# B and C rows of a selective scan: a BF16 scratch, two DMA queues, and an earlier dt

## What is computed

```python
xz = ln(x) @ in_proj_w.T
x_ssm, z = split(xz)                      # 2048 x 2048 each
xc = silu(causal_conv4(x_ssm) + conv_b)
xp = xc @ x_proj_w.T                      # one dt column, 16 of B, 16 of C
dt = softplus(xp[dt] * dt_proj_w + dt_proj_b)
dA = exp(dt * A)                          # 16 states per channel
h_t = dA_t * h_(t-1) + dt_t * B_t * xc_t  # along the 2048 time steps
y_t = sum over the 16 states of h_t * C_t
x = x + ln((y + xc * D) * silu(z) @ out_proj_w.T)
```

## Time and profile before

| | us |
|---|---|
| median of 3 runs | 8227.46 |
| lowest, highest | 8202.73, 8426.81 |
| the profiled execution | 8207.39 |
| its span on the slowest cores (2 and 4) | 8205.8 |
| its span on the fastest core (5) | 8162.0 |

### The profile page before, as it was taken

How to read it: one execution, slowest core, us unless ns; L and a number is a source line. 1 busy time by engine, 2 the same in 40 slices (tenths; PEclk the granted TensorE clock), 3 DMA queues, 4 the chain that set the end, 5 groups by cost and what they waited for, 6 DMA issues and landing times.

```text
span 8205.8 us, 45336 instructions; the slowest of 8 cores (8162.0 to 8205.8 us)
## 1 busy us (share of the span) xinstructions
PE 2813.7 (34%) x10928; PEld 1131.5 (14%) x11136; DVE 3911.4 (48%) x5726; ACT 1984.8 (24%) x2902; POOL 338.7 (4%) x639
## 2 busy tenths in 40 slices
PE   6200011001100020002605666666665645647272
PEld 3000000000000000001202222222221212223131
DVE  7199945996299917995212222122211343331414
ACT  4132212332133212332203333333331000011112
POOL 0100010001000010000000000000000000000000
PEclk9655556555655565555858777777776777768686
DMA  2600062001600070002691111111111111111211
GB/s 64 49 2 0 0 55 33 0 0 23 66 0 0 0 76 13 0 0 60 82 113 21 18 21 21 21 12 20 21 16 36 52 41 58 45 60 62 72 58 51
DMA packets 112654, 275.76 MB, mean 34 GB/s; under 512 B 19144, under 2 KB 39624, under 8 KB 111116
## 3 DMA queue, kind: packets, MB, share of 16 engines
q0 software_dynamic: 69200, 178.17, 16.4%
q1 hardware_dynamic: 33980, 77.91, 3.1%
q10 hardware_dynamic: 9216, 16.78, 0.6%
HBM read 339.04 MB, written 63.51 MB: 49 GB/s over the span
## 4 chain that ended last, share of the span: by engine, by line
DVE 33%; PE 30%; issue 11%; DMA 9%; another core or an unknown queue 8%; ACT 7%; DVEq 1%; ACTq 1%; SPq 0%; POOL 0%; POOLq 0%
DVE h_band L715 15%; PE psF L1337 7%; PE psF L1571 6%; DVE h_band L727 4%; PE psF L1352 4%; ACT attT L1382 4%; PE psF L1370 3%; PE psF L1770 3%; PE psF L1782 3%; DMA wvG<-wv 2%; DVE h_band L736 2%; DVE xc_a L1623 2%; DMA wzD<-winp_z 1%; PE psF L908 1%
## 5 line engine op out<-in xcount | busy, mean ns | idle before, releaser
L715 DVE TENSOR_TENSOR_SCAN h_band<-daD,hcol,dxD 128x512 f16<-128x512 f32 x1024 | 1302.5, 1277 | 2.3
L626 ACT ACTIVATE daD<-dtD,c_A 128x512 f32<-128x512 f32 x1024 | 732.2, 721 | 1828.9 <-DVE h_band L715 1818.8
L593 PE MATMUL psA<-woD,xc_a 128*128 128x512 bf16 x250 | 69.6, 400 | 2759.6 <-DVE xc_a L765 2728.0
L1382 ACT ACTIVATE attT<-psF 128x1024 bf16<-128x1024 f32 x512 | 523.9, 1023 | 871.5 <-PE psF L1352 870.3
L1337 PE MATMUL psF<-wvG,act_a 128*128 128x512 bf16 x1971 | 601.3, 459 | 245.6 <-DMA wvG<-wv 236.0
L1352 PE MATMUL psF<-qT_aug,kT_aug 65*128 65x512 bf16 x1024 | 376.3, 455 | 448.0 <-ACT attT L1382 439.9
L1418 DVE TENSOR_TENSOR vgt<-psF,gv_tm 128x512 bf16<-128x512 f32 x256 | 176.6, 690 | 680.1 <-PE psF L1337 672.9
L1571 PE MATMUL psF<-xc_a 128*128 128x512 bf16 x2002 | 469.7, 396 | 34.6 <-DVE xc_a L1623 31.9
L710 DVE TENSOR_TENSOR dxD<-uD,bb_sb 128x512 bf16<-128x512 bf16 x960 | 408.0, 425 | 95.6 <-DVE h_band L715 2.8
L1439 DVE TENSOR_TENSOR ost<-psF,rlbG 64x512 bf16<-64x512 f32 x64 | 43.7, 683 | 793.9 <-DMA rlbG<-lrow 793.9
L593 PEld LDWEIGHTS psA<-woD,xc_a 128*128 128x128 bf16 x256 | 22.2, 100 | 2805.1 <-issue 2789.7
(11 more groups left out here) (219 smaller groups left out, 3762.8 us busy)
## 6 DMA issues: line engine op xcount, KB each, us to landing
xc_a<-wob POOLq DMA_DIRECT2D x128, 256.0 KB, 4.6
wzD<-winp_z POOLq DMA_DIRECT2D x64, 256.0 KB, 3.9
woD<-woutT POOLq DMA_DIRECT2D x64, 256.0 KB, 4.8
wob<-wo POOLq DMA_DIRECT2D x1, 16384.0 KB, 301.3
wvG<-wv POOLq DMA_DIRECT2D x32, 512.0 KB, 9.1
xc_a<-w1b POOLq DMA_DIRECT2D x64, 256.0 KB, 6.2
xc_a<-w2b ACTq DMA_DIRECT2D x64, 256.0 KB, 7.6
xreD<-xin SPq DMA_DIRECT2D x16, 512.0 KB, 26.7
```

Of the source, the lines that this page charges most:

```text
L626: inc(s.activation(daD[n % 2][:], dt[:], AF.Exp, scale=c_A[:, dc * NN + n: dc * NN + n + 1]), "da")
L715: last = v.tensor_tensor_scan(h_band[:, n * TW:(n + 1) * TW], daD[n % 2][:], dxD[n % 2][:], hcol[:, dc * NN + n: dc * NN + n + 1], op0=OP. ...
L1382: inc(s.activation(attT[:, (2 * grp) * 512:(2 * grp + 2) * 512], psF1[:, 0:1024], AF.Exp, scale=0.125), "gs")
```

## The change

The scratch `xp_d` and its staging tiles become BF16. The 16 C loads of a slice leave GpSimd's queue and go to SP's, with a semaphore of their own, `gbs`: those of slice 0 at the head of SP's work, those of slice `tc + 1` behind SP's last store of slice `tc`, behind a wait that the scans of `tc` are done. VectorE waits for `gbs` as well. On ScalarE the loop over chunks is cut into `dt_only` and `da_loop`; dt of the next slice's chunk 0, with its wait for `gb`, goes ahead of the epilogue of the present slice, and that chunk's `da_loop` stays behind the silus of the next slice. The load of `dtr_b` stays on GpSimd and now turns BF16 into float32.

```diff
-    d_xpd = nc.dram_tensor("xp_d", [65, S], F32, kind="Internal").ap()
+    d_xpd = nc.dram_tensor("xp_d", [65, S], BF16, kind="Internal").ap()
...
-    xpstg = [sbb(f"xpstg{i}", [128, 512], F32) for i in range(2)]
+    xpstg = [sbb(f"xpstg{i}", [128, 512], BF16) for i in range(2)]
...
             for n in range(NN):
                 dma(gp, "gb", bb_sb[:, n * TW:(n + 1) * TW],
                     repl_ap(d_xpd[n:n + 1, :], TW, off_elems=tc * TW))
-                dma(gp, "gb", cb_sb[:, n * TW:(n + 1) * TW],
-                    repl_ap(d_xpd[32 + n:33 + n, :], TW, off_elems=tc * TW))
...
-            for dc in range(DC):
-                gidx = tc * DC + dc
+            def dt_only(ttc, dc):
+                gidx = ttc * DC + dc
                 if dc == 0:
-                    wge(s, "gb", QG_TCB[tc])
+                    wge(s, "gb", QG_TCB[ttc])
                 dt = dtD[dc % 2]
                 if gidx >= 2:
                     wge(s, "scv", (gidx - 1) * NN)
...
+            def da_loop(ttc, dc):
+                dt = dtD[dc % 2]
                 for n in range(NN):
-                    gn = gni(tc, dc, n)
+                    gn = gni(ttc, dc, n)
...
+            if tc > 0:
+                da_loop(tc, 0)
+            for dc in range(0 if tc == 0 else 1, DC):
+                dt_only(tc, dc)
+                da_loop(tc, dc)
+            if tc + 1 < TC:
+                dt_only(tc + 1, 0)
             for q in range(4):
...
+        def cb_repl(tc):
+            if tc >= 1:
+                wge(sync, "scv", tc * DC * NN)
+            for n in range(NN):
+                dma(sync, "gbs", cb_sb[:, n * TW:(n + 1) * TW],
+                    repl_ap(d_xpd[32 + n:33 + n, :], TW, off_elems=tc * TW))
+            QS_TCB[tc] = cnt["gbs"]
+        cb_repl(0)
         QS_RELOAD[0] = dma(sync, "xr", xreD[:], d_x[0:128, :])
...
                 dma(sync, "ssr", d_srcsp[i * 128:(i + 1) * 128, :], srcbD[:])
                 QS_SRCSP[i] = cnt["ssr"]
+            if tc + 1 < TC:
+                cb_repl(tc + 1)
...
             wge(v, "gb", QG_TCB[tc])
+            wge(v, "gbs", QS_TCB[tc])
```

More of the change, by code:

```diff
@@ L197, in _build @@
     mksem("qc", "qga", "qcx", "ax0", "ax1", "bw0", "bw1", "gb",
-          "wz0", "wz1", "wo0", "wo1", "wo2", "xps", "sx0", "sx1", "ssr", "xr",
+          "wz0", "wz1", "wo0", "wo1", "wo2", "xps", "gbs", "sx0", "sx1", "ssr", "xr",
           "t", "v", "s", "eps", "vf", "sf",
@@ L663, in _build @@
     QS_SRCSP = [0] * (TC * 4)
+    QS_TCB = [0] * TC
     @block.sync
@@ L811, in _ @@
             for nm in ["qc", "qga", "qcx", "ax0", "ax1", "bw0", "bw1", "gb",
-                       "wz0", "wz1", "wo0", "wo1", "wo2", "xps", "sx0", "sx1",
+                       "wz0", "wz1", "wo0", "wo1", "wo2", "xps", "gbs", "sx0", "sx1",
                        "ssr", "xr"]:
```

## The result

| | before | changed |
|---|---|---|
| median, us | 8240.4 | 8084.4 |
| lowest, us | 8194.3 | 8035.3 |
| profiled execution, span of the slowest core | 8205.8 | 8036.4 |
| first uD of slice 0 (all DMAs of the start behind it) | 415.40 | 363.01 |
| last scan work of slice 0 to first scan of slice 1 | 219.3 | 182.1 |

A forecast was written before the change was run, and what follows sets the result against it. Bound: trains of replicated B and C row loads, 3.15 us each, at the start and slice boundaries. Savings of 64 us at three boundaries (192) plus 59 at the start, 251 off 8207.4, gave 7956 us, range 7845 to 8150.

The forecast's parts named there:

- The bound: Start and slice boundaries: z weights wait behind 33 row loads in one queue, 3.15 us each, slow because of their source.
- d = 1.6 us: Time of one 128 KB B or C row load after the change: read rate of 86 GB/s stays, with half the bytes.
- the rival of the full rate: Row loads run at full rate, d = 0.55 us, the pace of the issue; 355 us saved, 7852 us; chance 0.25.
- the rival of the unchanged row: A row load costs the same whatever its length, d = 3.15 us; 63 us saved, 8144 us; chance 0.29.
- The start: Slice 0: 17 loads take 41 us, z starts at 294 for 356.5; 62 us less 3 for C loads, 59 saved.
- The epilogue in series: Boundary: epilogue starts behind the 17 B loads, from 1155.6 to 1196, 40 us long since its reloads are free again.
- The z tiles: Boundary, behind the epilogue: 50.5 us in the old timeline less one round of 6.5, 44 us, plus 6 for C loads.
- this sign of its own: Stated sign of being wrong: C loads beside the z tiles stretch them by more than 15 us.
- the overhang: Boundary: C loads (26 us) and z weights (about 20) need 46 to 55 us of engines against 46 of z tiles.
- The sum: One boundary: first scan at 1248 for 1311.95, 64 us saved, three times 192; with the start's 59, 251 us.
- the forecast's own case: Whole kernel with d between 1.2 and 2.3 us: 7917 to 8035 us; chance 0.38.
- The stated range: Whole kernel: 7845 to 8150 us, from the full-rate rival to the unchanged-row rival, leaving out the slower case.

The follow-up runs named there:

- the different rows: Kernel before, with each B and C load reading 128 different rows of a float32 weight instead of one scratch row 128 times; ratio 0.959 to before.
- the second comparison: The changed kernel measured once more against the kernel before, beside the last experiments on one chip; ratio 0.978 (0.9758 to 0.9802).
- four copies: Changed kernel with its BF16 scratch stored four times, each of four neighbouring partitions reading another copy; ratio 0.967 to before.

## Why the prediction was right, and where it was off

**The bound.** That the z weights stand behind 33 loads in one queue, and that a load is slow because of its source, was right. The reason given, engines busy at a low rate, was only an argument; the different rows showed it.

**d = 1.6 us.** Right in size: 1.65 us in the kernel with the scratch alone, 1.8 us in the two trains together at the start, and at a boundary 33 us for 17 loads, landing and the last out-projection weight ahead of them included. The read rate of some 80 GB/s (128 KB in 1.65 us) did stay, and the rival of the full rate and that of the unchanged row both fell. By the Trainium skill (DMA: Bandwidth & Descriptors, the anatomy of one SWDGE DMA), which fits 2.0 us plus bytes over 436 GB/s, the bytes of one such load would need an estimated 0.3 us. The trace does not agree: they took 1.65, and the loads from 128 different rows still 0.93.

**The start.** 52 us for 59. Weights at 298.7 for 294, because a load took 1.8 us and not 1.6; that SP's queue would pass half a load for each of GpSimd's came true (between eight and nine for 17). The C loads still under way held the z tiles 5 us longer, where 3 were put (60.6 us, 298.7 to 359.4, for 55.2).

**The epilogue in series.** Right in each part: it starts some 26 us after the out-projection (22.8 summed), is 40 us long, and its reloads are on time. What the prediction did not do is to ask what this order costs against the alternative. It counted the early dt as 2.4 us gained and took the epilogue's place behind the loads as given; taken out, it gives 13, 12 and 9 us back at the three boundaries, and put in alone it costs 32 us in all.

**The z tiles: the step that failed.** The prediction put 44 us for the tiles and 6 us for the C loads beside them; measured are 51 and 20, 71.4 us in all. The prediction had said that it would be wrong if the C loads stretched the z tiles by more than 15 us, and by this sign of its own it was. Of the 21 us missing at the first boundary 7 are a miscount: the 50.5 us of the old timeline begin with the first silu, when the first pair of tiles was already done, so no round could be taken off for it. The other 14 are the C loads. The prediction added up how long the engines are busy, found 46 to 55 us of work for a 46 us stage, and charged the overhang. (Its 20 us for the z weights, 0.17 us a row, stands in no row; the earlier trace rows gives the 29 us that it has as the upper bound. With them the overhang is 9 us, not the 20 measured.) But the z tiles are not a load on the engines, they are a chain: load a pair, multiply, load the next. Each link pays for what is in the queues at that moment: two links waited 13.9 and 10.7 us, and 2.7 and 2.8 us without the C loads. The DMA queues from 1150 to 1184 us, SP's (the C loads) and GpSimd's:

```profile
q1 hardware_dynamic: 2402, 2.27, 65.2%
q0 software_dynamic: 420, 0.78, 15.7%
```

While they ran, the C loads took most of the engines' time, and still the engines were not busy all through: what the tiles waited for was the landing of single loads. The Trainium skill's section Issuing engines are not separate DMA queues (DMA: Bandwidth & Descriptors) says that the queues interleave on the same engines. The trace agrees: a z weight that lands in 3.7 us alone took up to 16.0 beside SP's loads.

**The sum.** At the first boundary 64 us were forecast; 21 us for the z tiles and 4 for the B loads are to be taken off, which leaves 39, and 37 were measured. From first scan to first scan the later two saved 43 and 46 us. With 52 for the start that is 178 us, against 3868.9 - 3692.0 = 177 in the two profiles. The ratio 0.9824 is worth some 145 us, and the medians of the second comparison differ by 177.

**What the range owes to its width.** The profiled execution of the changed kernel took 8037.9 us, just above the 7917 to 8035 of the forecast's own case (d between 1.2 and 2.3), though d was in the middle of it. The stated range holds because it reaches on to the rival of the unchanged row, which did not come true.

## What to carry to other kernels

A long train of loads that each read one short row for all 128 partitions can run far below the rate of the same loads from different rows, and here it took time about in proportion to the row's bytes: look at what the queue moves while the engines are busy, then halve the bytes, spread the row over copies, or load it while the engines are idle. An in-order engine that is given an early piece of work is also given that work's wait: ask what stands behind it. A transfer laid beside a chain of small double-buffered loads costs each link of the chain its queueing time: here 20 us, where the engines' time added up had said 6.

## What the runs showed of the hardware

A 128-partition load of one float32 row of 2 KB, cast to BF16, took 3.15 us (some 80 GB/s read); the same load from 128 different rows took 0.93 us (some 280 GB/s). One BF16 row of 1 KB, which needs no cast, took 1.65 us. With four copies the z weights stood 23.6 us behind the loads, with one copy 46 us, both in two queues. Why one place is read so slowly these runs do not say; that four places help speaks for a limit where the bytes lie, not at the reading engines, and the fast layernorm rows show that it does not hold for every row. SP's issue of 16 such loads took 45 us at the start, and 20 us with four copies, where it has 0.55 us for one: how fast SP can issue went with how fast the loads drained. That a full queue holds its engine is the likely reading; the traces do not show the fill.
